# Graph block on one core: bringing the weighted sums back by a scaled reflection on VectorE instead of a transpose and a product on TensorE

## The chip, the core and the metric

The kernel runs on one core of a Trainium2 chip. The metric is the device time of one execution in microseconds. The times given are medians of several runs.

## The reference

64 independent graphs (`B` = 64) of 128 nodes with 128 features each go through two layers. Cut to what matters:

```python
# layer 0, for every pair (i, j) of nodes
h = relu(hi[:, :, None, :] + hj[:, None, :, :] + b1)      # hi = x W1[:H], hj = x W1[H:]
y = einsum('bijk,kl->bijl', h, W2) + b2
y = layernorm(y) * gamma + beta
out0 = einsum('bij,bijh->bih', adj, y)
x1 = layernorm(x + out0)
# layer 1: attention
Wh = x1 @ Ww.T + Wb
s = (Wh @ aw[:C])[:, :, None] + (Wh @ aw[C:])[:, None, :] + ab
e = exp(s) * adj;  alpha = e / sum(e)
x2 = layernorm(x1 + alpha @ x1)
```

Most of the work is the product of 128 x 128 pairs with `W2` for each graph.

## The kernel before

**Slots.** The kernel is a software pipeline of 66 slots. Slot t does three things at once: the pairs of graph t (`pairs`), the weighted sums of graph t-1 (`gather`) and the tail of graph t-2 (`tail`: residual, first layer norm, attention, second layer norm, store); it also prepares graph t+1 (`prep`). The first 12 slots are written out, then a loop of five turns has a body of 10 slots, and the last 4 are written out again (`run_slots`, lines 152 to 161). Each engine runs the same slots in an order written out by hand; semaphores join them. No planner is involved. SyncE's queue issues the loads and stores (lines 181 to 197).

**Units and quarts.** A slot has 16 units, and a unit has two quarts (k = 0 to 31 in a slot), each of four of the 128 rows i. For a unit GpSimd adds the two hidden halves to `h` (line 260), ScalarE applies the relu in place (line 289), two units ahead of the copies, TensorE multiplies each row by `w_pair` into a bank of `y_ps` (lines 606 to 615, a helper `mm` at line 531 issues one product over four column groups, 8 matmul records each), ScalarE copies the quart to `y` (line 371), and VectorE multiplies bank and copy and accumulates the sum of squares in `q` (line 521). `y_ps` has `YRING` = 5 banks, so TensorE begins quart k only when `q_done` tells that quart k-5 is through (line 612).

**The basis.** `w_pair` maps to a basis (a reflection) in which the mean over features falls away: 127 columns carry the centred vector, and the last is the product with the centred second bias. In `y` the last column holds a constant 2, so the squares in line 521 give the variance with the bias in it, and the last column of the weighted sums is twice the sum of the weights, by which the bias comes back. The sums are therefore also in that basis: 32 products of 512 columns, in 8 chunks issued behind the units named in `SUM_AT` (4, 6, 7, 9, 10, 12, 13, 15), land in `agg_ps`.

**The tail before.** VectorE combines the four parts of `agg_ps` to `o_sb` in four steps (lines 450 and 454, unit 0). TensorE transposes it at unit 3 (line 591), ScalarE copies the transpose to `oT_sb` at unit 3 (line 335), and TensorE multiplies by `w_back` at unit 5 (line 594), which brings it back to 128 features with gamma applied. VectorE adds `x_beta` (line 461, unit 5) to get `x1p`, then takes statistics. The rest follows at units 7 (normalise and the two scores), 9 (exponential, scaled copy), 11 (attention product and its use), 12 and 14 (second layer norm). Preparation of the next graph has transposes at unit 7, copies at unit 9, and products and `project` at unit 11.

In the VectorE loop a unit has four places e = 0 to 3, and after each place follow two squares: places 0 and 1 belong to the unit's first quart, 2 and 3 to its second. So place (1, 3) is ahead of the last two squares of quart 3. The steps that the prediction names by a pair (unit, place) are in the function that starts at line 428.

Of the kernel before, what the change touches and what calls it, by code (L numbers as in the profile page):

```python
# [33 lines left out]
def gnn_pair_kernel(nc, x, adj, W1, b1, W2, b2, gamma, beta, Ww, Wb, aw, ab, out):  # L34
# [22 lines left out]
    CHUNK = 4  # L57
# [5 lines left out]
    with ctx:  # L63
# [18 lines left out]
        basis, basis_half = sb("basis", [K, K]), sb("basis_half", [K, K])  # L82
        b2c, b2c_rep = sb("b2c", [K, 1]), sb("b2c_rep", [K, S])
        gdiag = sb("gdiag", [K, K])
        a1rep, a2rep, wbrep, a12 = sb("a1rep", [K, S]), sb("a2rep", [K, S]), sb("wbrep", [K, S]), sb("a12", [K, 1])
        w_pair = sb("w_pair", [K, K])
        w_back = sb("w_back", [K, K])
# [24 lines left out]
        o_sb, oT_sb = sb("o_sb", [S, K]), sb("oT_sb", [K, S])  # L112
# [14 lines left out]
        x2p = att_ps[:, 3 * K:4 * K]  # L127

# [13 lines left out]
        agg_done, o_part, o_stored, oT_ps_s, oT_sb_s, f_ps_s = sem("agg_done"), sem("o_part"), sem("o_stored"), sem("oT_in_psum"), sem("oT_in_sbuf"), sem("f_in_psum")  # L142
# [126 lines left out]
        def _(act):  # L269
# [37 lines left out]
            def slot(t, half, p, pairs, prep, gather, tail, early, first_bank):  # L307
                for u in range(UNITS):
# [69 lines left out]
        def _(dve):  # L378
# [28 lines left out]
            nc.vector.tensor_copy(basis_half[:, 0:LAST], basis[:, 0:LAST]).then_inc(s_setup_dve, 1)  # L407
            nc.vector.tensor_scalar(basis_half[:, LAST:S], basis[:, LAST:S], 0.5, None, ALU.mult).then_inc(s_setup_dve, 1)
# [12 lines left out]
            dve.wait_ge(s_setup_pe, 8)  # L421
            nc.vector.tensor_copy(bnorm[:], att_ps[:, 1:2]).then_inc(s_ready, 1)
            nc.vector.tensor_copy(w_pair[:], agg_ps[:, 0:K]).then_inc(s_ready, 1)
            nc.vector.tensor_copy(w_back[:], agg_ps[:, K:2 * K]).then_inc(s_ready, 1)
            dve.wait_ge(s_ready, 6)
            dve.wait_ge(s_part, 1)

            def slot(t, half, p, pairs, prep, gather, tail, early, first_bank):

                for u, e in ((u, e) for u in range(UNITS) for e in range(2 * QPU)):  # L430
# [13 lines left out]
                    if tail and (u, e) == (0, 0):  # L444

                        dve.wait_ge(agg_done, (t - 1) * CHUNKS)
                        if early >= 3:

                            dve.wait_ge(oT_ps_s, t - 2)
# [12 lines left out]
                    if tail and (u, e) == (5, 1):  # L462
                        dve.wait_ge(x1p_ready, t - 1)
                        nc.vector.bn_stats(st1[:], x1p).then_inc(st1_ready, 1)
                    if tail and (u, e) == (5, 2):
# [4 lines left out]
                    if tail and (u, e) == (7, 0):  # L470
# [3 lines left out]
                    if tail and (u, e) == (7, 1):  # L474
                        nc.vector.tensor_tensor_reduce(out=s_terms[:, 1, :], in0=x1p, in1=v1row[:], scale=rs1[:, 0:1], scalar=0.0,
                                                       op0=ALU.mult, op1=ALU.add, accum_out=s_ij[:, 0:1]).then_inc(si_ready, 1)
                    if tail and (u, e) == (7, 2):
                        nc.vector.tensor_tensor_reduce(out=s_terms[:, 0, :], in0=x1p, in1=v2row[:], scale=rs1[:, 0:1], scalar=score_c[:, 0:1],
                                                       op0=ALU.mult, op1=ALU.add, accum_out=s_ij[:, 1:2]).then_inc(sj_ready, 1)
                    if prep and (u, e) == (11, 0):  # L480
# [4 lines left out]
                    if tail and (u, e) == (11, 0):  # L485
# [3 lines left out]
                    if tail and (u, e) == (11, 1):  # L489
                        dve.wait_ge(z_e_ready, t - 1)  # L490
                        nc.vector.reciprocal(z_r, z_e).then_inc(z_r_ready, 1)
                    if tail and (u, e) == (11, 2):
                        dve.wait_ge(z_r_ready, t - 1)
                        nc.vector.tensor_scalar(rz[:], z_r, e_ij[:, 0:1], None, ALU.mult).then_inc(rz_ready, 1)
                    if tail and (u, e) == (11, 3):
# [4 lines left out]
                    if tail and (u, e) == (12, 0):  # L500
                        dve.wait_ge(x2p_ready, t - 1)
                        nc.vector.bn_stats(st2[:], x2p).then_inc(st2_ready, 1)
                    if tail and (u, e) == (12, 1):
# [4 lines left out]
                    if tail and (u, e) == (14, 0):  # L508
# [22 lines left out]
        def _(pe):  # L531
# [38 lines left out]
            mm(agg_ps[:, K:2 * K], basis_half[:], gdiag[:]).then_inc(s_setup_pe, 1)  # L570


            pe.wait_ge(s_ready, 6)
# [76 lines left out]
```

## Time and profile before

| | |
|---|---|
| median of 3 runs | 2393.05 us (2391.15 to 2393.16) |
| profiled execution | 2389.61 us |
| its span, first to last instruction | 2387.6 us |
| mean granted clock of TensorE | 0.996 |
| TensorE busy | 2349.4 us (98%), 73280 matmul records |
| VectorE busy | 2108.2 us (88%) |
| ScalarE busy | 2200.3 us (92%) |
| GpSimd busy | 2015.2 us (84%) |
| DMA engines, mean share | below 10% in every slice |

The profile is of one execution. Busy time is the union of an engine's instructions; instructions of one engine can overlap, so the distance from one start to the next can be smaller than a duration. A wait is idle time of an engine together with what ended it; "issue" means that the profile shows nothing that it waited for. Timelines give start, duration, engine, line and operation, with neighbours of one kind merged into one row.

### The profile page before, as it was taken

How to read it: one execution, taken by the hardware profiler on the slowest of the kernel's cores; microseconds unless marked ns; L12 is line 12 of the kernel's file. 1: busy time of each engine (PE TensorE's matmuls, PEld its weight loads, DVE VectorE, ACT ScalarE, POOL GpSimd, SP SyncE). 2: the span in 40 equal slices, each digit the busy share in tenths (PEclk: the TensorE clock that was granted, in tenths of full speed). 3: DMA queues.
4: the chain of work that ended last, by engine and by line, in shares of the span. 5: the costliest groups of instructions: out<-in, count | busy, mean ns of one | idle time of the engine just before them, and what ended most of it. 6: DMA issues, size and time to landing. Idle time of an engine off the chain costs nothing.

```text
span 2387.6 us, 179792 instructions
## 1 busy us (share of the span) xinstructions
PE 2349.4 (98%) x73280; PEld 2118.9 (89%) x73280; DVE 2108.2 (88%) x17881; ACT 2200.3 (92%) x3841; POOL 2015.2 (84%) x1227
## 2 busy tenths in 40 slices
PE   8999999999999999999999999999999999999997
PEld 7888888899898899889889889989999889999996
DVE  7898998888898888888889899888898888888897
ACT  7999999999999899999899999989999989999996
POOL 8888888888888888888788888888888878888884
PEclk9999999999999999999999999999999999999999
DMA  0000000000000000000000000000000000000000
GB/s 20 10 15 16 10 16 16 11 16 16 11 16 10 17 16 10 16 12 15 17 11 16 14 12 16 11 17 16 11 16 12 15 17 10 16 16 10 16 9 11
DMA packets 48651, 33.06 MB, mean 14 GB/s; under 512 B 6208, under 2 KB 47808, under 8 KB 47808
## 3 DMA queue, kind: packets, MB, share of 16 engines
q1 hardware_dynamic: 46512, 21.12, 3.2%
q8 instruction: 590, 9.67, 1.7%
q14 instruction: 253, 2.07, 0.3%
q10 hardware_dynamic: 1296, 0.20, 0.0%
HBM read 17.11 MB, written 4.19 MB: 9 GB/s over the span
## 4 chain that ended last, share of the span: by engine, by line
PE 96%; ACT 2%; DVE 1%; issue 1%; POOL 0%; ACTq 0%; DMA 0%; DVEq 0%
PE y_ps L535 74%; PE agg_ps L580 18%; PE prep_ps L535 4%; ACT y L271 1%; ACT h L289 1%; PE att_ps L535 1%; DVE squares L521 0%; POOL h L260 0%; DMA beta_rows<-in_L_gnn_beta_dram 0%; DVE o_sb L454 0%; DVE q L521 0%; POOL wz L251 0%; ACT x1s L354 0%; DVE x1e L472 0%; DVE att_ps L498 0%
## 5 line engine op out<-in xcount | busy, mean ns | idle before, releaser
L260 POOL TENSOR_TENSOR h<-bT,aT 128x1024 f32<-128x1024 f32 x1024 | 1942.4, 1916 | 319.2 <-PE y_ps L535 303.6
L521 DVE CUSTOM_DVE_ANT_0 squares<-y_ps,y 128x128 bf16<-128x128 f32 x8192 | 1848.8, 285 | 219.9 <-ACT y L271 199.2
L535 PEld LDWEIGHTS y_ps<-w_pair,h 128*32 128x32 f32 x65536 | 1894.0, 110 | 160.3 <-issue 108.0
L535 PE MATMUL y_ps<-w_pair,h 128*32 128x128 f32 x65536 | 1961.6, 273 | 17.1 <-issue 11.5
L271 ACT ACTIVATE y<-y_ps 128x508 f32<-128x508 f32 x2048 | 1142.8, 598 | 138.0 <-PE y_ps L535 130.6
L289 ACT ACTIVATE h<-h 128x1024 f32<-128x1024 f32 x1024 | 1092.0, 1066 | 18.3 <-POOL h L260 15.9
L521 DVE DVE_READ_ACCUMULATOR2_ANT q<- 128x1 f32 x8192 | 678.6, 83 | 0.0
L580 PE MATMUL agg_ps<-y,wz 128*32 128x512 f32 x4096 | 583.8, 592 | 0.0
L580 PEld LDWEIGHTS agg_ps<-y,wz 128*32 128x32 f32 x4096 | 173.6, 110 | 3.4 <-issue 3.0
L454 DVE SCALAR_TENSOR_TENSOR o_sb<-agg_ps,part,o_sb 128x128 f32<-128x128 f32 x192 | 66.5, 347 | 0.2
L234 POOL TENSOR_TENSOR wz<-adjT,rstd 128x128 f32<-128x128 f32 x64 | 34.4, 538 | 33.4 <-ACT rstd L323 33.4
L535 PEld LDWEIGHTS prep_ps<-ident,x_in 128*32 128x32 f32 x512 | 26.4, 110 | 29.1 <-issue 23.3
L513 DVE TENSOR_SCALAR x_out<-att_ps,mv,rs 128x128 f32<-128x128 f32 x64 | 26.2, 410 | 28.1 <-ACT rs L360 28.1
L535 PEld LDWEIGHTS prep_ps<-w_back,oT_sb 128*32 128x32 f32 x512 | 26.1, 110 | 27.4 <-issue 20.2
L535 PEld LDWEIGHTS prep_ps<-xT,w1a 128*32 128x32 f32 x512 | 26.4, 111 | 26.1 <-issue 20.3
L246 POOL TENSOR_TENSOR x_beta<-beta_part,x_res 128x128 f32<-128x128 f32 x64 | 29.4, 460 | 9.8 <-ACT beta_part L329 9.8
L535 PE MATMUL att_ps<-x1s,adjS 128*32 128x129 f32 x512 | 32.4, 276 | 3.6 <-ACT x1s L354 3.5
L535 PE MATMUL prep_ps<-ident,o_sb 128*32 128x128 f32 x512 | 31.4, 273 | 4.3 <-DVE o_sb L454 4.3
L535 PE MATMUL prep_ps<-ident,x_in 128*32 128x128 f32 x512 | 32.2, 275 | 3.1 <-DMA x_in<-in_x_dram 3.1
L535 PE MATMUL prep_ps<-w_back,oT_sb 128*32 128x128 f32 x512 | 32.0, 273 | 0.4 <-ACT oT_sb L271 0.4
L535 PE MATMUL prep_ps<-ident,adj_in 128*32 128x128 f32 x512 | 32.2, 275 | 0.0
L535 PE MATMUL prep_ps<-xT,w1b 128*32 128x128 f32 x512 | 32.2, 275 | 0.0
(89 smaller groups left out, 709.9 us busy)
## 6 DMA issues: line engine op xcount, KB each, us to landing
x_in<-in_x_dram SPq DMA_DIRECT2D x64, 64.0 KB, 2.6
adj_in<-in_adj_dram SPq DMA_DIRECT2D x64, 64.0 KB, 2.6
x_res<-in_x_dram SPq DMA_DIRECT2D x64, 64.0 KB, 2.1
adj_res<-in_adj_dram SPq DMA_DIRECT2D x64, 64.0 KB, 2.0
out_dram<-x_out SPq DMA_DIRECT2D x64, 64.0 KB, 1.8
w<-in_L_gnn_W_dram ACTq DMA_DIRECT2D x1, 64.0 KB, 2.4
w1a<-in_L_gnn_W_dram SPq DMA_DIRECT2D x1, 64.0 KB, 2.2
w1b<-in_L_gnn_W_dram SPq DMA_DIRECT2D x1, 64.0 KB, 2.3
```

What stands on the lines that cost most here:

```text
L234: nc.gpsimd.tensor_tensor(columns, adjT[:, 1 - p, :].rearrange("j (g c s) -> j g c s", g=GROUPS, s=CHUNK), rstd[:].rearrange("j (c s g) -> ...
L246: nc.gpsimd.tensor_tensor(x_beta[:], beta_part[:], x_res[:, p, :], ALU.add).then_inc(x_beta_ready, 1)
L260: nc.gpsimd.tensor_tensor(h[:, u % HRING].rearrange("k (r g) s -> k r g s", g=GROUPS), bT[:, p, :].unsqueeze(1).unsqueeze(1).broadcast_to( ...
L271: return nc.scalar.activation(dst, src, ACT.Copy)
L289: nc.scalar.activation(h[:, u % HRING], h[:, u % HRING], ACT.Relu).then_inc(h_ready, 1)
L454: nc.vector.scalar_tensor_tensor(out=o_sb[:], in0=agg_ps[:, e * K:(e + 1) * K], scalar=part[:, e:e + 1], in1=o_sb[:], op0=ALU.mult, op1=AL ...
L513: nc.vector.tensor_scalar(x_out[:], x2p, mv2[:, 0:1], rs2[:, 0:1], ALU.subtract, ALU.mult).then_inc(out_ready, 1)
L521: last = nc.vector.tensor_tensor_reduce(out=squares[:, (first_bank + k) % YRING, n, :], in0=y_ps[(first_bank + k) % YRING][:, n, :], in1=y ...
L535: last = nc.tensor.matmul(dst[cols], lhsT[:, cols], rhs, start=True, stop=True, tile_position=(0, g * GROUP))
L580: last = nc.tensor.matmul(agg_ps[g * GROUP:(g + 1) * GROUP, :], wz[:, g, chunk, :], y_chunk[:, :, g, :], start=(chunk == 0), stop=(chunk = ...
```

## The change

The sums are brought back on VectorE. The basis is a reflection, so going back is the vector itself, plus multiples of two fixed row vectors: the product with gamma (`gamma_rows`, whose last column is zero), `mean_rows` times the sum of the row (`o_sum`), and `bias_rows` times the last column. The fourth combining step writes to PSUM (`o_all`, the place of `x2p`) and also accumulates `o_sum`. Three steps follow at (1, 1), (1, 2) and (1, 3), each waiting for the one before. The transpose, the copy `oT_sb`, the product by `w_back` and their semaphores go. The tail after that stands one unit earlier, preparation two units earlier (transposes at 5, copies at 7, products at 9), and setup builds the three row tiles instead of `w_back`.

```diff
@@ VectorE, setup @@
-            nc.vector.tensor_copy(basis_half[:, 0:LAST], basis[:, 0:LAST]).then_inc(s_setup_dve, 1)
-            nc.vector.tensor_scalar(basis_half[:, LAST:S], basis[:, LAST:S], 0.5, None, ALU.mult).then_inc(s_setup_dve, 1)
+            nc.vector.memset(gamma_rows[:, LAST:S], 0.0).then_inc(s_setup_dve, 1)
+            nc.vector.memset(o_sum[:], 0.0).then_inc(s_setup_dve, 1)
...
-            nc.vector.tensor_copy(w_back[:], agg_ps[:, K:2 * K]).then_inc(s_ready, 1)
-            dve.wait_ge(s_ready, 6)
+            nc.vector.tensor_copy(gamma_rows[:, 0:LAST], agg_ps[:, 2 * K:3 * K - 1]).then_inc(s_ready, 1)
+            nc.vector.tensor_scalar(mean_rows[:, 0:LAST], agg_ps[:, 2 * K:3 * K - 1], -1.0 / (K - sqrt(K)), None, ALU.mult).then_inc(s_ready, 1)
+            nc.vector.tensor_scalar(mean_rows[:, LAST:S], agg_ps[:, 3 * K - 1:3 * K], 1.0 / sqrt(K), None, ALU.mult).then_inc(s_ready, 1)
+            dve.wait_ge(s_ready, 8)
+            nc.vector.scalar_tensor_tensor(out=bias_rows[:], in0=agg_ps[:, K:2 * K], scalar=0.5, in1=mean_rows[:],
+                                           op0=ALU.mult, op1=ALU.subtract).then_inc(s_ready, 1)
+            dve.wait_ge(s_ready, 9)
@@ VectorE, slot @@
-                        nc.vector.scalar_tensor_tensor(out=o_sb[:], in0=agg_ps[:, e * K:(e + 1) * K], scalar=part[:, e:e + 1],
-                                                       in1=o_sb[:], op0=ALU.mult, op1=ALU.add).then_inc(
-                                                           o_stored if e == CHUNK - 1 else o_part, 1)
-
-                    if tail and (u, e) == (5, 0):
+                        if e < CHUNK - 1:
+                            nc.vector.scalar_tensor_tensor(out=o_sb[:], in0=agg_ps[:, e * K:(e + 1) * K], scalar=part[:, e:e + 1],
+                                                           in1=o_sb[:], op0=ALU.mult, op1=ALU.add).then_inc(o_part, 1)
+                        else:
+                            nc.vector.scalar_tensor_tensor(out=o_all, in0=agg_ps[:, e * K:(e + 1) * K], scalar=part[:, e:e + 1],
+                                                           in1=o_sb[:], op0=ALU.mult, op1=ALU.add,
+                                                           accum_out=o_sum[:, 0:1]).then_inc(o_stored, 1)
+                    if tail and (u, e) == (1, 1):
+                        dve.wait_ge(o_stored, t - 1)
+                        nc.vector.tensor_tensor(x1p, o_all, gamma_rows[:], ALU.mult).then_inc(scaled_ready, 1)
+                    if tail and (u, e) == (1, 2):
+                        dve.wait_ge(scaled_ready, t - 1)
+                        nc.vector.scalar_tensor_tensor(out=x1p, in0=mean_rows[:], scalar=o_sum[:, 0:1], in1=x1p,
+                                                       op0=ALU.mult, op1=ALU.add).then_inc(mean_added, 1)
+                    if tail and (u, e) == (1, 3):
+                        dve.wait_ge(mean_added, t - 1)
+                        nc.vector.scalar_tensor_tensor(out=x1p, in0=bias_rows[:], scalar=o_all[:, LAST:S], in1=x1p,
+                                                       op0=ALU.mult, op1=ALU.add).then_inc(bias_added, 1)
+
+                    if tail and (u, e) == (4, 0):
                         dve.wait_ge(x_beta_ready, t - 1)
-                        dve.wait_ge(f_ps_s, t - 1)
-                        nc.vector.tensor_tensor(x1p, tail_ps[:, 1, :], x_beta[:], ALU.add).then_inc(x1p_ready, 1)
+                        dve.wait_ge(bias_added, t - 1)
+                        nc.vector.tensor_tensor(x1p, x1p, x_beta[:], ALU.add).then_inc(x1p_ready, 1)
@@ ScalarE, slot @@
-                    if tail and u == 3:
-                        act.wait_ge(oT_ps_s, t - 1)
-                        if early >= 3:
-
-                            act.wait_ge(f_ps_s, t - 2)
-                        copy(oT_sb[:], tail_ps[:, 0, :]).then_inc(oT_sb_s, 1)
-                    if tail and u == 7:
+                    if tail and u == 6:
...
-                    if prep and u == 9:
+                    if prep and u == 7:
...
-                    if tail and u == 9:
+                    if tail and u == 8:
...
-                    if tail and u == 14:
+                    if tail and u == 13:
@@ TensorE, slot @@
-                    if tail and u == 3:
-                        pe.wait_ge(o_stored, t - 1)
+                    if prep and u == 5:
                         if gather:
 
                             pe.wait_ge(ln_v_ready, t)
-                        mm(tail_ps[:, 0, :], o_sb[:], ident[:]).then_inc(oT_ps_s, 1)
-                    if tail and u == 5:
-                        pe.wait_ge(oT_sb_s, t - 1)
-                        mm(tail_ps[:, 1, :], oT_sb[:], w_back[:]).then_inc(f_ps_s, 1)
-                    if prep and u == 7:
-                        if tail:
-
-                            pe.wait_ge(x1p_ready, t - 1)
                         prep_transposes(t + 1, 1 - p, nth16(half, p, 1), True)
-                    if prep and u == 11:
+                    if prep and u == 9:
                         prep_products(t + 1)
-                    if tail and u == 11:
+                    if tail and u == 10:
```

The other VectorE places move with them: statistics from unit 5 to 4, normalisation and scores from 7 to 6, `project` from 11 to 9, the use of the attention product from 11 to 10, the second statistics from 12 to 11, the output from 14 to 13.

## Rows read from the trace of the kernel before

**Rows 1.** The page: busy time by engine; shares of the chain of waits.
```profile
PE 2349.4 (98%) x73280; PEld 2118.9 (89%) x73280; DVE 2108.2 (88%) x17881; ACT 2200.3 (92%) x3841; POOL 2015.2 (84%) x1227
...
PE 96%; ACT 2%; DVE 1%; issue 1%; POOL 0%; ACTq 0%; DMA 0%; DVEq 0%
```

**Rows 2.** Waits, whole run: total us, times, longest us.
```profile
DVE squares L521 <- ACT y L271: 199.2, 467, 4.3
...
PEld y_ps L535 <- DVE q L521: 15.1, 47, 3.1
```

**Rows 3.** Timeline of TensorE's matmuls in one slot: start us, us, then the instruction.
```profile
1002.68 5.43 PE L535 MATMUL y_ps<-w_pair,h 128*32 128x128 f32 x192
1007.92 0.41 PE L535 MATMUL prep_ps<-ident,o_sb 128*32 128x128 f32 x8
1008.13 3.68 PE L535 MATMUL y_ps<-w_pair,h 128*32 128x128 f32 x128
...
1012.49 0.41 PE L535 MATMUL prep_ps<-w_back,oT_sb 128*32 128x128 f32 x8
1012.71 3.68 PE L535 MATMUL y_ps<-w_pair,h 128*32 128x128 f32 x128
...
1039.02 3.25 PE L535 MATMUL y_ps<-w_pair,h 128*32 128x128 f32 x112
```

**Rows 4.** Timeline of VectorE in the same slot, quarts 1 to 4.
```profile
1006.49 0.34 DVE L454 SCALAR_TENSOR_TENSOR o_sb<-agg_ps,part,o_sb 128x128 f32<-128x128 f32 x1
1006.75 0.28 DVE L521 CUSTOM_DVE_ANT_0 squares<-y_ps,y 128x128 bf16<-128x128 f32 x1
...
1008.85 0.28 DVE L521 CUSTOM_DVE_ANT_0 squares<-y_ps,y 128x128 bf16<-128x128 f32 x1
1009.05 0.08 DVE L521 DVE_READ_ACCUMULATOR2_ANT q<- 128x1 f32 x1
1009.53 0.29 DVE L521 CUSTOM_DVE_ANT_0 squares<-y_ps,y 128x128 bf16<-128x128 f32 x1 [0.39 <-ACT y L271]
```

**Rows 5.** VectorE, same slot: steps like the new ones; then a group.
```profile
1015.28 0.29 DVE L461 TENSOR_TENSOR att_ps<-prep_ps,x_beta 128x128 f32<-128x128 f32 x1
1015.50 0.29 DVE L521 CUSTOM_DVE_ANT_0 squares<-y_ps,y 128x128 bf16<-128x128 f32 x1
...
1020.86 0.41 DVE L478 CUSTOM_DVE_ANT_0 s_terms<-att_ps,v2row,score_c 128x128 f32<-128x128 f32 x1
1021.19 0.08 DVE L478 DVE_READ_ACCUMULATOR2_ANT s_ij<- 128x1 f32 x1
...
L498 DVE SCALAR_TENSOR_TENSOR att_ps<-att_ps,rz,x1e 128x128 f32<-128x128 f32 x64 | 22.7, 354 | 0.1
```

**Rows 6.** Timeline: a read that releases TensorE in slot 0; later, a weight load.
```profile
26.90 0.08 DVE L521 DVE_READ_ACCUMULATOR2_ANT q<- 128x1 f32 x1
27.03 1.75 PEld L535 LDWEIGHTS y_ps<-w_pair,h 128*32 128x32 f32 x64 [0.16 <-DVE q L521]
...
1007.81 0.24 PEld L535 LDWEIGHTS prep_ps<-ident,o_sb 128*32 128x32 f32 x8
```

**Rows 7.** Timeline of TensorE and VectorE in a slot near 898 us.
```profile
897.52 2.89 PE L535 MATMUL y_ps<-w_pair,h 128*32 128x128 f32 x96
...
898.49 0.08 DVE L521 DVE_READ_ACCUMULATOR2_ANT q<- 128x1 f32 x1
```

**Rows 8.** Timeline of TensorE and VectorE in the slot after a loop turn.
```profile
1195.02 3.68 PE L535 MATMUL y_ps<-w_pair,h 128*32 128x128 f32 x128
...
1194.78 0.08 DVE L521 DVE_READ_ACCUMULATOR2_ANT q<- 128x1 f32 x1
```

**Rows 9.** Timeline of VectorE: the last read of quart 8.
```profile
1014.44 0.08 DVE L521 DVE_READ_ACCUMULATOR2_ANT q<- 128x1 f32 x1
```

**Rows 10.** Timeline of VectorE in the first of the two last tails.
```profile
2367.44 0.27 DVE L442 TENSOR_REDUCE adj_sum<-adj_res 128x1 f32<-128x128 f32 x1
2369.22 0.30 DVE L461 TENSOR_TENSOR att_ps<-prep_ps,x_beta 128x128 f32<-128x128 f32 x1 [1.50 <-PE prep_ps L535]
```

More of the change, by code:

```diff
@@ L81, in gnn_pair_kernel @@
         house, centre = sb("house", [K, K]), sb("centre", [K, K])
-        basis, basis_half = sb("basis", [K, K]), sb("basis_half", [K, K])
+        basis = sb("basis", [K, K])
         b2c, b2c_rep = sb("b2c", [K, 1]), sb("b2c_rep", [K, S])
         gdiag = sb("gdiag", [K, K])
+        gamma_rows, mean_rows, bias_rows = sb("gamma_rows", [S, K]), sb("mean_rows", [S, K]), sb("bias_rows", [S, K])
         a1rep, a2rep, wbrep, a12 = sb("a1rep", [K, S]), sb("a2rep", [K, S]), sb("wbrep", [K, S]), sb("a12", [K, 1])
         w_pair = sb("w_pair", [K, K])
-        w_back = sb("w_back", [K, K])
         v1row, v2row = sb("v1row", [S, K]), sb("v2row", [S, K])
@@ L111, in gnn_pair_kernel @@
         part = sb("part", [S, CHUNK])
-        o_sb, oT_sb = sb("o_sb", [S, K]), sb("oT_sb", [K, S])
+        o_sb, o_sum = sb("o_sb", [S, K]), sb("o_sum", [S, 1])
         x1e = sb("x1e", [S, K + 1])
@@ L127, in gnn_pair_kernel @@
         x2p = att_ps[:, 3 * K:4 * K]
+        o_all = x2p
         s_w, s_w1 = sem("weights_loaded"), sem("first_layer_weights_loaded")
@@ L141, in gnn_pair_kernel @@
         v_ready, ln_v_ready, rstd_ready, w_ready, adjS_ready = sem("v_ready"), sem("ln_v_ready"), sem("rstd_ready"), sem("w_ready"), sem("adjS_ready")
-        agg_done, o_part, o_stored, oT_ps_s, oT_sb_s, f_ps_s = sem("agg_done"), sem("o_part"), sem("o_stored"), sem("oT_in_psum"), sem("oT_in_sbuf"), sem("f_in_psum")
+        agg_done, o_part, o_stored = sem("agg_done"), sem("o_part"), sem("o_stored")
+        scaled_ready, mean_added, bias_added = sem("scaled_by_gamma"), sem("mean_part_added"), sem("bias_part_added")
         x1p_ready, st1_ready, mv1_ready, ln1_ready, rs1_ready = sem("x1p_ready"), sem("st1_ready"), sem("mv1_ready"), sem("ln1_ready"), sem("rs1_ready")
@@ L419, in _ @@
             nc.vector.tensor_tensor(score_c[:], setup_ps[:, 3, 0:1], abc[:], ALU.add).then_inc(s_ready, 1)
-            dve.wait_ge(s_setup_pe, 8)
+            dve.wait_ge(s_setup_pe, 9)
             nc.vector.tensor_copy(bnorm[:], att_ps[:, 1:2]).then_inc(s_ready, 1)
             nc.vector.tensor_copy(w_pair[:], agg_ps[:, 0:K]).then_inc(s_ready, 1)
-            nc.vector.tensor_copy(w_back[:], agg_ps[:, K:2 * K]).then_inc(s_ready, 1)
-            dve.wait_ge(s_ready, 6)
+            nc.vector.tensor_copy(gamma_rows[:, 0:LAST], agg_ps[:, 2 * K:3 * K - 1]).then_inc(s_ready, 1)
[5 more added lines that the diff above has]
+            dve.wait_ge(s_ready, 9)
             dve.wait_ge(s_part, 1)
@@ L446, in slot @@
                         dve.wait_ge(agg_done, (t - 1) * CHUNKS)
-                        if early >= 3:
-                            dve.wait_ge(oT_ps_s, t - 2)
                         nc.vector.tensor_scalar(o_sb[:], agg_ps[:, 0:K], part[:, 0:1], None, ALU.mult).then_inc(o_part, 1)
@@ L462, in slot @@
-                    if tail and (u, e) == (5, 1):
+                        dve.wait_ge(bias_added, t - 1)
+                        nc.vector.tensor_tensor(x1p, x1p, x_beta[:], ALU.add).then_inc(x1p_ready, 1)
+                    if tail and (u, e) == (4, 1):
                         dve.wait_ge(x1p_ready, t - 1)
                         nc.vector.bn_stats(st1[:], x1p).then_inc(st1_ready, 1)
-                    if tail and (u, e) == (5, 2):
+                    if tail and (u, e) == (4, 2):
                         dve.wait_ge(st1_ready, t - 1)
@@ L469, in slot @@
                         nc.vector.bn_aggr(mv1[:], st1[:]).then_inc(mv1_ready, 1)
-                    if tail and (u, e) == (7, 0):
+                    if tail and (u, e) == (6, 0):
                         dve.wait_ge(rs1_ready, t - 1)
                         nc.vector.tensor_scalar(x1e[:, 0:K], x1p, mv1[:, 0:1], rs1[:, 0:1], ALU.subtract, ALU.mult).then_inc(x1_ready, 1)
-                    if tail and (u, e) == (7, 1):
+                    if tail and (u, e) == (6, 1):
                         nc.vector.tensor_tensor_reduce(out=s_terms[:, 1, :], in0=x1p, in1=v1row[:], scale=rs1[:, 0:1], scalar=0.0,
                                                        op0=ALU.mult, op1=ALU.add, accum_out=s_ij[:, 0:1]).then_inc(si_ready, 1)
-                    if tail and (u, e) == (7, 2):
+                    if tail and (u, e) == (6, 2):
                         nc.vector.tensor_tensor_reduce(out=s_terms[:, 0, :], in0=x1p, in1=v2row[:], scale=rs1[:, 0:1], scalar=score_c[:, 0:1],
                                                        op0=ALU.mult, op1=ALU.add, accum_out=s_ij[:, 1:2]).then_inc(sj_ready, 1)
-                    if prep and (u, e) == (11, 0):
+                    if prep and (u, e) == (9, 0):
                         if early >= 1:
@@ L484, in slot @@
                         project(t + 1, 1 - p)
-                    if tail and (u, e) == (11, 0):
+                    if tail and (u, e) == (10, 0):
                         dve.wait_ge(att_done, t - 1)
@@ L488, in slot @@
                         nc.vector.tensor_scalar(z_e, att_ps[:, K:K + 1], e_ij[:, 0:1], None, ALU.mult).then_inc(z_e_ready, 1)
-                    if tail and (u, e) == (11, 1):
+                    if tail and (u, e) == (10, 1):
                         dve.wait_ge(z_e_ready, t - 1)
                         nc.vector.reciprocal(z_r, z_e).then_inc(z_r_ready, 1)
-                    if tail and (u, e) == (11, 2):
+                    if tail and (u, e) == (10, 2):
                         dve.wait_ge(z_r_ready, t - 1)
                         nc.vector.tensor_scalar(rz[:], z_r, e_ij[:, 0:1], None, ALU.mult).then_inc(rz_ready, 1)
-                    if tail and (u, e) == (11, 3):
+                    if tail and (u, e) == (10, 3):
                         dve.wait_ge(rz_ready, t - 1)
@@ L499, in slot @@
                                                        op0=ALU.mult, op1=ALU.add).then_inc(x2p_ready, 1)
-                    if tail and (u, e) == (12, 0):
+                    if tail and (u, e) == (11, 0):
                         dve.wait_ge(x2p_ready, t - 1)
                         nc.vector.bn_stats(st2[:], x2p).then_inc(st2_ready, 1)
-                    if tail and (u, e) == (12, 1):
+                    if tail and (u, e) == (11, 1):
                         dve.wait_ge(st2_ready, t - 1)
@@ L507, in slot @@
                         nc.vector.bn_aggr(mv2[:], st2[:]).then_inc(mv2_ready, 1)
-                    if tail and (u, e) == (14, 0):
+                    if tail and (u, e) == (13, 0):
                         dve.wait_ge(rs2_ready, t - 1)
@@ L569, in _ @@
             mm(agg_ps[:, 0:K], w2T[:], basis[:]).then_inc(s_setup_pe, 1)
-            mm(agg_ps[:, K:2 * K], basis_half[:], gdiag[:]).then_inc(s_setup_pe, 1)
-            pe.wait_ge(s_ready, 6)
+            mm(agg_ps[:, K:2 * K], b2c_rep[:], gdiag[:]).then_inc(s_setup_pe, 1)
+            mm(agg_ps[:, 2 * K:3 * K], ones[:], gdiag[:]).then_inc(s_setup_pe, 1)
+            pe.wait_ge(s_ready, 9)
             def weighted_sums(b_parity, chunk):
```

## The prediction

> **What bounds the kernel now.** I read the busy shares and the chain of waits first [rows 1], then the table of who waited for whom [rows 2], then one steady slot as a timeline, TensorE first [rows 3], then VectorE [rows 4].
>
> TensorE is busy for 98% of the span and makes 96% of the chain [rows 1]. Its own waits for VectorE are small: 15.1 us of weight loads held by `q` [rows 2]. The slot of 1002.68 to 1039.02 takes 36.34 us [rows 3]. In it 24 block products of `y_ps` run from 1002.68 to 1007.92, so one block product (8 matmul records) costs 5.24 / 24 = 0.218 us, and a quart of four costs 0.873 us. The two products that the change removes stand in that slot at 1007.92 (0.21 us to the next) and 1012.49 (0.22 us) [rows 3]. So the slot is filled by TensorE, and work taken out of it is worth its full time, as long as nothing else is late.
>
> The reader has to see what could be late. The ring has 5 banks: quart k may start only when VectorE has finished the squares of quart k-5 (`q_done`, line 612). VectorE needs four squares at 0.21 us, 0.84 us a quart, against 0.873 us on TensorE. In units 0 to 3 there are no weighted sums on TensorE (`SUM_AT` begins at 4), so VectorE cannot catch up there, and just there it has the extra steps at the slot's start. From 1006.49 to 1009.05 it starts one instruction after the other with no idle time, and only before 1009.53 does it wait, 0.39 us, for ScalarE's copy of `y` [rows 4].
>
> Quart 3's last accumulator read is at 1009.05 and lasts 0.08, ends 1009.13 [rows 4]. Quart 8, which waits for it, starts at 1008.13 + 2 x 0.873 = 1009.88 [rows 3]. The slack is 0.75 us. Quart 9 starts at 1010.75, and quart 4, from 1009.53, ends 0.84 + 0.08 later, at 1010.46: slack 0.29 us.
>
> **What is removed.** Per tail two block products, 0.218 + 0.218 = 0.437 us of TensorE: the first stood before quart 6, the second before quart 10. Over the 62 slots that have both a tail and pairs (2 to 63) this is 27 us, if nothing takes their place. ScalarE's copy to `oT_sb` goes too; I cost it at nothing, because quart 8 waits for VectorE work that has no ScalarE wait in front of it.
>
> **What is added.** Three VectorE steps at (1,1), (1,2), (1,3), all ahead of the end of quart 3's squares. What counts is the distance from one start to the next. The product with `gamma_rows`: line 461 has the same kinds of operands, and the squares follow it 0.22 us later (1015.28 to 1015.50) [rows 5]. The two scalar_tensor_tensor: the one at 1006.49 is followed 0.26 us later (1006.75) [rows 4]. Sum 0.22 + 0.26 + 0.26 = 0.74 us. Two things have no row. The fourth weighted-sum step now also accumulates `o_sum`; squares accumulate at 0.21 us, so nearly nothing is expected, and the ends are 0 and the read's 0.08. The last step takes its scalar from PSUM; a second pointer made line 478 0.33 (1020.86 to 1021.19), 0.07 over 0.26 [rows 5], so its ends are 0 and 0.07. I take 0.77, with ends 0.63 (three at the 0.21 of a square) and 0.94 (0.77 plus both, rounded).
>
> The Trainium skill, "VectorE: DVE Perf Modes", section "The DRAIN you can't avoid", speaks against the change: it says that the next operation does not start until the pipe is empty. By that rule each step would cost its whole duration; the rival below prices it. The rows disagree so far: 0.35 long, the next start 0.26 later.
>
> **The new wait.** Quart 3's squares end 0.77 later, and quart 8 is ready 0.218 earlier. A stalled quart also needs time to begin: after the read of 26.90 ended at 26.98 the weight load started at 27.03, 0.05 later, and a matmul follows its load by 0.11 (load at 1007.81 [rows 6], matmul at 1007.92 [rows 3]); 0.16 together. Stall before quart 8: 0.77 + 0.218 + 0.16 - 0.75 = 0.40 us. Quart 9 adds nothing: quart 4's squares can start at 1009.05 + 0.77 = 1009.82 rather than 1009.53, end 0.29 later at 1010.75, and quart 9 in its new place, 1009.88 - 0.218 + 0.40 + 0.873 = 1010.93, is later than that by 0.18. Queued behind the stalled quart on TensorE is everything else of the slot, so the stall counts in full.
>
> The slot then changes by -0.437 + 0.40 = -0.04 us. In other slots the slack is smaller: in the one around 898 us, 60 of the 64 records of quarts 6 and 7 are left at 897.52, so quart 8 starts at 897.52 + 60 x 0.0273 = 899.16, and the read ends at 898.57 (0.0273 is 0.218 / 8) [rows 7]: slack 0.59, stall 0.56, the slot 0.12 us longer. Some slots have TensorE late on its own queue, which the new stall partly swallows. I take the 57 ordinary slots (62 less the five after a loop turn) at zero.
>
> The first slot after each of the five loop turns is different: quart 8 starts at 1195.02 + 1.746 = 1196.77 and the read ends at 1194.86 [rows 8], slack 1.9 us. No stall; these give the whole 0.437: 2.2 us.
>
> **What is moved.** Statistics, scores, preparation and attention go one or two units earlier on all engines together, and the transposes now stand before quart 10, giving 0.437 us there that they take back at 14. The first step that they could hurt is quart 13: it starts at 1012.71 + 2.62 = 1015.33 and needs the read of 1014.44, ended 1014.52 [rows 9], slack 0.8. TensorE is there 0.40 us later than before (the removed 0.437 returned by the transposes, plus the stall) and two of the moved steps add some 0.4 us before that read, of which VectorE's wait hides a part. So it stays at 0.8. From there on a weighted sum stands between most quarts, and the slack grows. I cost the moves at nothing; if that cover went, they would cost the 0.4 us. No DMA is issued differently, but the loads of `x_in` and `adj_in` on SyncE's queue start earlier, since they wait for the transposes; their data is needed a slot later.
>
> Setup: one more product and about 0.7 us more of VectorE before TensorE's first quart. The first squares wait for ScalarE and GpSimd anyway; nothing. The last two tails: `x1p` came at 2369.22, 1.78 us after the reduction began at 2367.44 [rows 10]. Now it follows that reduction by three dependent steps of some 0.4 us: 0.3 us less at best.
>
> **Sum.** 0 + 2.2 + 0.3 = 2.5 us less. The profiled execution took 2389.61, a span of 2387.6 and 2.0 around it; the median of the runs is 2393.05, 0.14% above, and I take the difference over unchanged: 2390.5 us.
>
> **The rivals.**
> A, the whole 27 us arrives: it needs VectorE's delay to disappear before quart 3 ends. 62 x 0.437 = 27, so 2366. For it: TensorE is 98% busy. Against it: VectorE's unbroken row of starts [rows 4]. Chance 0.07.
> B, the steps are cheap, near 0.63 us: stall 0.26, 0.18 x 57 = 10 and 2.5, so 2380.5. Chance of a gain over 4.8 us this way 0.15.
> C, slower: the steps hold VectorE for as long as their bars are. One of line 498 lasts 0.354 [rows 5], line 461's 0.29: 0.29 + 0.35 + 0.35 = 1.0 us, stall 0.63, the slot 0.19 us longer, 57 x 0.19 = 11 less the 2.5: 2401.5. It decides for slower by 0.2% once the three cost more than 0.90 us. With the dear ends only (0.94) it gives 0.13 x 57 - 2.5 = 5, 2398. It is what the rule of the Trainium skill on the drain ("VectorE: DVE Perf Modes", "The DRAIN you can't avoid") would do here. Chance 0.20.
> D, the change does not do what it says, since the new place of `x1s` or of the moved copies on ScalarE makes TensorE wait later in the slot: 0.2 us a slot would be 11 us, 2402. Nothing in units 8 to 15 is that close. Chance 0.02.
>
> **How the numbers follow.** A measurement of this kernel tells about 0.2%, 4.8 us, from no change. The forecast, within that of the old time, has 0.56, A and B 0.22, C and D 0.22. The range takes in the ends of the step costs, B and C: 2380 to 2402. It leaves out A.
>
> **What would show it.** After the change: the two products gone and the quarts still at 0.873 us; the three steps 0.22 and 0.26 apart from what follows; a new wait of TensorE for `q` before quart 8, some 0.3 to 0.5 us, in most slots; slots of about 36.3 us, those after a turn 0.4 us shorter. If the wait is absent and slots are 35.9, A is right. If the steps' spacing is 0.3 to 0.35, C. The prediction is wrong in its working if slots are shorter or longer by a wait in another place.

## The result, and the profile after

The changed kernel takes 2374.19 us (2370.8 to 2379.49, 5 runs); the kernel before 2391.15 us (2386.97 to 2393.16, 5 runs). The ratio is 0.9935, interval 0.9916 to 0.9953: faster by 0.65%, about 15 us. The prediction of 2390.5 us, range 2380 to 2402, was wrong, and the time lies below its range. The profiled execution of the changed kernel took 2375.56 us, span 2373.6, clock 0.995; before 2389.61 and 2387.6. The spans differ by 14.0 us. The five executions of the changed kernel lie up to 8.7 us apart, so what follows from one profiled execution of each kernel holds to a few us in all; only the floors defined below repeat to 0.01 us.

The page, as in [rows 1]:

```profile
PE 2328.1 (98%) x72264; PEld 2008.4 (85%) x72264; DVE 2147.3 (90%) x18140; ACT 2191.7 (92%) x3777; POOL 2017.4 (85%) x1227
...
PE 76%; DVE 16%; issue 5%; ACT 3%; ACTq 0%; DMA 0%; DVEq 0%
```

VectorE has moved into the chain, from 1% to 16%. The table of waits alone does not show the new wait: weight loads held by `q` went from 15.1 us, 47 times [rows 2], to 43.9 us, 140 times, but the kernel without the three steps, tried below, has 50.4 us, 170 times, and no wait before quart 8. The timeline shows it.

One steady slot of the changed kernel on TensorE (timeline: start us, us, instruction), to set beside [rows 3]:

```profile
997.68 9.20 PE L548 MATMUL y_ps<-w_pair,h 128*32 128x128 f32 x320
1006.69 1.04 PE L594 MATMUL agg_ps<-y,wz 128*32 128x512 f32 x8
...
1033.87 2.37 PE L548 MATMUL y_ps<-w_pair,h 128*32 128x128 f32 x80
```

The slot takes 1033.87 - 997.68 = 36.19 us. Its first 320 records, ten quarts, take 9.01 us until the weighted sum; at 0.873 us a quart they would take 8.73. So 0.28 us of waiting lie in there, 0.26 before quart 8 and 0.02 behind it. VectorE in the same slot, to set beside [rows 4]:

```profile
1001.49 0.35 DVE L456 SCALAR_TENSOR_TENSOR att_ps<-agg_ps,part,o_sb 128x128 f32<-128x128 f32 x1
1001.76 0.14 DVE L456 DVE_READ_ACCUMULATOR att_ps<-agg_ps,part,o_sb 128x1 f32 x1
1001.76 0.28 DVE L534 CUSTOM_DVE_ANT_0 squares<-y_ps,y 128x128 bf16<-128x128 f32 x1
...
1002.80 0.29 DVE L461 TENSOR_TENSOR att_ps<-att_ps,gamma_rows 128x128 f32<-128x128 f32 x1
1003.00 0.28 DVE L534 CUSTOM_DVE_ANT_0 squares<-y_ps,y 128x128 bf16<-128x128 f32 x1
...
1003.42 0.35 DVE L464 SCALAR_TENSOR_TENSOR att_ps<-mean_rows,o_sum,att_ps 128x128 f32<-128x128 f32 x1
1003.68 0.28 DVE L534 CUSTOM_DVE_ANT_0 squares<-y_ps,y 128x128 bf16<-128x128 f32 x1
...
1004.10 0.35 DVE L468 SCALAR_TENSOR_TENSOR att_ps<-bias_rows,att_ps 128x128 f32<-128x128 f32 x1
1004.36 0.28 DVE L534 CUSTOM_DVE_ANT_0 squares<-y_ps,y 128x128 bf16<-128x128 f32 x1
...
1004.78 0.08 DVE L534 DVE_READ_ACCUMULATOR2_ANT q<- 128x1 f32 x1
```

And TensorE just behind that read, its matmuls in one view and its weight loads in another:

```profile
1004.92 1.30 PE L548 MATMUL y_ps<-w_pair,h 128*32 128x128 f32 x40
...
1004.92 1.14 PEld L548 LDWEIGHTS y_ps<-w_pair,h 128*32 128x32 f32 x44 [0.34 <-DVE q L534]
```

The read ends at 1004.86, and quart 8 begins 0.06 us later. The wait is where the prediction put it.

**Where the 14.0 us went.** I measured every slot as the distance between the first matmuls of quart 0 in successive slots, and call the shortest slot of a kernel its floor. The loop has five turns, so it jumps back four times; each jump lengthens the slot that it ends and the one behind it, eight slots in all. The other 42 slots of the loop are ordinary, and what they have over the floor in all is called their gaps.

| us | before | after | difference |
|---|---|---|---|
| start, slots 0 and 1 | 84.5 | 84.7 | +0.2 |
| slots 2 to 11, written out | 363.4 | 363.1 | -0.4 |
| 42 ordinary slots of the loop | 1536.8 | 1520.9 | -15.9 |
| of these the floor, 42 x 36.343 and 42 x 36.185 | 1526.4 | 1519.8 | -6.6 |
| of these gaps | 10.4 | 1.1 | -9.3 |
| 8 slots at the jumps | 308.1 | 310.2 | +2.1 |
| end | 94.8 | 94.7 | -0.1 |

Two things stand out: the floor fell by 0.158 us instead of the 0.04 forecast for the steady slot, and the gaps are gone. In the kernel before, a gap looks like this on TensorE, here in three slots that are ten apart:

```profile
530.53 0.96 PE L535 MATMUL y_ps<-w_pair,h 128*32 128x128 f32 x27 [0.45 <-issue]
...
900.87 0.96 PE L535 MATMUL y_ps<-w_pair,h 128*32 128x128 f32 x27 [0.46 <-issue]
...
1271.09 0.96 PE L535 MATMUL y_ps<-w_pair,h 128*32 128x128 f32 x27 [0.17 <-issue]
```

All three stand behind the fourth of the 32 records of quart 9, at the same instruction of the loop body in three turns. Inside a quart the kernel has no wait, and the profile names none.

### The profile page after: what moved, and what is told of

The parts are those of the page before. It is cut to its first block, busy times and chain, and to the rows that moved or that the text cites. A ratio compares the mean times of both kernels' runs of the same rounds, so it can differ in the third digit from the quotient of the medians.

```text
span 2373.6 us, 177761 instructions
## 1 busy us (share of the span) xinstructions
PE 2328.1 (98%) x72264; PEld 2008.4 (85%) x72264; DVE 2147.3 (90%) x18140; ACT 2191.7 (92%) x3777; POOL 2017.4 (85%) x1227
## 4 chain that ended last, share of the span: by engine, by line
PE 76%; DVE 16%; issue 5%; ACT 3%; ACTq 0%; DMA 0%; DVEq 0%
PE y_ps L548 56%; PE agg_ps L594 16%; DVE squares L534 9%; PE prep_ps L548 2%; DVE q L534 2%; ACT y L273 2%; ACT h L291 1%; DVE att_ps L456 1%; DVE o_sb L453 1%; DVE att_ps L468 1%; DVE att_ps L464 1%; PE att_ps L548 1%; DVE o_sb L448 1%; DVE att_ps L461 0%; DVE adj_sum L443 0%
## 5 line engine op out<-in xcount | busy, mean ns | idle before, releaser
L548 PEld LDWEIGHTS y_ps<-w_pair,h 128*32 128x32 f32 x65536 | 1821.7, 110 | 263.0 <-issue 208.1
L548 PE MATMUL y_ps<-w_pair,h 128*32 128x128 f32 x65536 | 1922.5, 273 | 22.8 <-issue 13.9
L594 PE MATMUL agg_ps<-y,wz 128*32 128x512 f32 x4096 | 537.3, 592 | 2.8 <-DVE att_ps L456 2.8
L594 PEld LDWEIGHTS agg_ps<-y,wz 128*32 128x32 f32 x4096 | 127.9, 110 | 7.1 <-POOL wz L236 3.6
L548 PEld LDWEIGHTS att_ps<-x1s,adjS 128*32 128x32 f32 x512 | 17.8, 110 | 44.6 <-issue 35.5
L453 DVE SCALAR_TENSOR_TENSOR o_sb<-agg_ps,part,o_sb 128x128 f32<-128x128 f32 x128 | 44.3, 346 | 0.1
L437 DVE TENSOR_SCALAR prep_ps<-q,bnorm 128x128 f32<-128x128 f32 x64 | 22.6, 354 | 10.4 <-issue 8.2
L485 DVE TENSOR_SCALAR x1e<-att_ps,mv,rs 128x128 f32<-128x128 f32 x64 | 26.2, 410 | 3.9 <-ACT rs L337 1.9
L331 ACT ACTIVATE beta_part<-beta_rows,adj_sum 128x128 f32<-128x128 f32 x64 | 25.5, 398 | 3.8 <-DVE adj_sum L443 3.8
L350 ACT ACTIVATE x1s<-x1e,e_ij 128x129 f32<-128x129 f32 x64 | 25.9, 405 | 2.1
```

Source lines behind the costliest of these rows:

```text
L485: nc.vector.tensor_scalar(x1e[:, 0:K], x1p, mv1[:, 0:1], rs1[:, 0:1], ALU.subtract, ALU.mult).then_inc(x1_ready, 1)
L548: last = nc.tensor.matmul(dst[cols], lhsT[:, cols], rhs, start=True, stop=True, tile_position=(0, g * GROUP))
L594: last = nc.tensor.matmul(agg_ps[g * GROUP:(g + 1) * GROUP, :], wz[:, g, chunk, :], y_chunk[:, :, g, :], start=(chunk == 0), stop=(chunk = ...
```

## The experiments

Theories on the floor: the ring before quart 8 (the three steps delay quart 3's squares), against something else in the slot. Theories on the gaps: A, the new wait swallows them; B, they depend on TensorE's instructions, by their count, their place in the slot or their address; C, chance. Where only one execution is given, its sum of gaps is uncertain by 2 us or so (10.4 and 12.1 us in two executions of the kernel before).

### The kernel before once more

> The kernel before, looked at once more. In its first profile the 56 ordinary slots sum to 2051.8 us with a median slot of 36.34, so 16.5 us lie over the median, most of it gaps of TensorE that the profile puts to issue. Theory own queue (gaps belong to this program): about 10 to 17 us over the median again, most gaps before quarts 6 to 10. Rival chance (gaps differ from execution to execution): anything from 0 to 17, in other slots.

Span 2390.1 us. Gaps 12.1 us, jumps 307.3. The gaps belong to the program, and so do their places. To see where they fall I compared every ordinary slot with a usual one, matmul record by matmul record. In the first execution 21 stalls are longer than 0.15 us, 8.4 of the 10.4 us. They stand at nine places of the loop body, and eight of these show again in the second execution, as the one shown above does:

```profile
902.38 0.96 PE L535 MATMUL y_ps<-w_pair,h 128*32 128x128 f32 x27 [0.17 <-issue]
```

All 21 stand within 5 records of a regular grid, one place every 125 matmul records, counted from the start of the loop body; most places of the grid show none. Which turn has a stall, and how long it is, differs. Chance (C) falls.

### The change without its three steps

```diff
-                    if tail and (u, e) == (1, 1):
...
-                    if tail and (u, e) == (1, 3):
...
-                        dve.wait_ge(bias_added, t - 1)
-                        nc.vector.tensor_tensor(x1p, x1p, x_beta[:], ALU.add).then_inc(x1p_ready, 1)
+                        dve.wait_ge(o_stored, t - 1)
+                        nc.vector.tensor_tensor(x1p, o_all, x_beta[:], ALU.add).then_inc(x1p_ready, 1)
```

> The changed kernel without the three VectorE steps; leaves out bringing the sums back. Ring theory: the wait before quart 8 goes and the median slot is 35.90 (36.34 less 0.437). If another step of the slot held the changed kernel, the slot stays at 36.2. On the gaps of TensorE's own queue: theory A, the wait before quart 8 swallows them: they come back here, some 10 us over the median, span about 2361. Theory B, they went with the fewer TensorE instructions or with their place in memory: they stay away, span about 2351.

2359.28 us, ratio 0.9853 (0.9834 to 0.9871), span 2356.0. Floor 35.91: the three steps are the whole of what holds the changed kernel above the full removal, and the ring theory stands. The span lies midway between the two forecasts, 2361 and 2351; the gaps decide. They are 1.1 us, with no wait before quart 8. So no wait swallowed them, and A falls.

### The kernel before with three steps

```diff
...
+                    if tail and (u, e) == (1, 1):
+                        nc.vector.tensor_tensor(x1p, x2p, ones[:], ALU.mult).then_inc(d1_ready, 1)
+                    if tail and (u, e) == (1, 2):
+                        dve.wait_ge(d1_ready, t - 1)
+                        nc.vector.scalar_tensor_tensor(out=x1p, in0=ident[:], scalar=part[:, 0:1], in1=x1p,
+                                                       op0=ALU.mult, op1=ALU.add).then_inc(d2_ready, 1)
+                    if tail and (u, e) == (1, 3):
+                        dve.wait_ge(d2_ready, t - 1)
+                        nc.vector.scalar_tensor_tensor(out=x1p, in0=ident[:], scalar=x2p[:, LAST:S], in1=x1p,
+                                                       op0=ALU.mult, op1=ALU.add).then_inc(d3_ready, 1)
...
```

> The kernel before with three VectorE steps of the same forms put at (1,1), (1,2), (1,3); their result is not used. Both products on TensorE stay. Ring theory: quart 3 ends 0.73 later against a slack of 0.75 to 0.71 and a wake-up of 0.06 to 0.15, so a wait of 0.05 to 0.15 before quart 8 and slots of 36.40 to 36.50, up to 6 us more in all. Theory A (a wait swallows gaps): TensorE now has no slack to lose, gaps before quarts 6 to 8 hurt less, 16.5 over the median becomes 8 or less, span 2381 to 2386. Theory B: the gaps stay, span 2391 to 2395.

2397.32 us, ratio 1.0007 (0.9997 to 1.0018), span 2395.5. The floor is 36.47 in the written-out slots and 36.39 in the loop, as the ring theory gave. Gaps 14.3 us although there is a wait, if a short one: A falls from this side too, and the span is half a microsecond above B's range.

### The steps spread

```diff
-                    if tail and (u, e) == (1, 1):
+                    if tail and (u, e) == (2, 0):
...
-                    if tail and (u, e) == (1, 2):
+                    if tail and (u, e) == (3, 0):
...
-                    if tail and (u, e) == (1, 3):
+                    if tail and (u, e) == (4, 0):
...
-                    if tail and (u, e) == (4, 0):
+                    if tail and (u, e) == (4, 1):
```

(The statistics follow at (4, 2) and (4, 3).)

> The changed kernel with the same three steps at (2,0), (3,0), (4,0), where VectorE waits for ScalarE's copy anyway, and the addition and statistics one place later, (4,1) to (4,3). Ring theory: quart 3 is no longer delayed, quart 4 by nothing (0.22 fits in its 0.47 us of idle time), so the wait before quart 8 goes; quart 9 is left with 0.29 - 0.218 = 0.07 us; median slot 35.90 to 36.00, 11 to 16 us less than the changed kernel in all. If the count of steps and not their place matters, the slot stays at 36.2. With theory A on the gaps the span is about 2361 to 2364, with B 2351 to 2358.

2361.69 us, ratio 0.9856 (0.9838 to 0.9874), span 2360.6, floor 35.91, gaps 4.4. The span is 13.0 us below that of the changed kernel, as the ring theory said, but above B's range of 2351 to 2358; against the kernel without the steps, 3.3 of the 4.6 us more are gaps. The same three steps cost nothing on the floor when VectorE would be idle. TensorE in one slot:

```profile
991.30 8.92 PE L548 MATMUL y_ps<-w_pair,h 128*32 128x128 f32 x320
1000.04 1.04 PE L594 MATMUL agg_ps<-y,wz 128*32 128x512 f32 x8
```

Ten quarts in 8.74 us: no wait is left. VectorE in the same slot shows why:

```profile
997.68 0.30 DVE L461 TENSOR_TENSOR att_ps<-att_ps,gamma_rows 128x128 f32<-128x128 f32 x1
998.15 0.29 DVE L534 CUSTOM_DVE_ANT_0 squares<-y_ps,y 128x128 bf16<-128x128 f32 x1 [0.17 <-ACT y L273]
```

The first step ends inside VectorE's wait for ScalarE's copy, and 0.17 us of it are still over.

### Two products put back into the changed kernel

```diff
+                    if tail and u == 3:
+                        pe.wait_ge(o_stored, t - 1)
+                        if gather:
+                            pe.wait_ge(ln_v_ready, t)
+                        if pairs:
+                            pe.wait_ge(ab_sb_s, t + 1)
+                        mm(prep_ps[:, 0, :], ones[:], ident[:])
+                    if tail and u == 5:
+                        mm(prep_ps[:, 1, :], ones[:], ident[:])
```

> The changed kernel with two products on TensorE put back at units 3 and 5 (on constants, result unused). Ring theory: quart 8 comes 0.218 later against the same VectorE, so the wait of 0.26 shrinks to 0.04 to 0.13; shortest slot 36.38 to 36.47. Gaps in TensorE's own queue (excess of the 42 slots of the loop body that are not at a jump, over the shortest slot: 10.5 and 12.3 in two looks at the kernel before, 1.3 in the changed one): theory count or place of the products says they return, 8 to 14; theory address says they stay near 1 or land anywhere, since the code around is not that of before.

2402.71 us, one run; span 2400.7. Floor 36.41, gaps 11.8 (expected 8 to 14). The products bring the gaps back. The slots written out are at 36.5 and longer, 366.5 us for the ten, and the jumps take 311.9, so this is slower than either kernel.

### Two products at other units

In the kernel with the spread steps:

```diff
+                    if tail and u in (12, 14):
+                        if prep:
+                            pe.wait_ge(ab_sb_s, t + 2)
+                        mm(prep_ps[:, 0, :], ones[:], ident[:])
```

> The kernel with the spread steps, and two products on TensorE put back, but at units 12 and 14. Shortest slot 35.91 + 0.437 = 36.35. Theory count (more instructions in a slot or in the loop body make the gaps): excess 8 to 14 as before. Theory place (the gaps come since products stand in the long run of quarts without weighted sums, units 0 to 4): excess 1 to 5, as without them.

2389.08 us, one run; span 2386.9. Floor 36.35, gaps 8.3, against 4.4 without the products. They come back although the products are far from the long run of quarts. The theory of place in the slot falls, count stays.

### Code shifted

```diff
             prep_transposes(0, 0, 16, False)
+            for _ in range(10):
+                mm(y_ps[0][:, 0, :], ident[:], ident[:])
```

In the kernel before:

> The kernel before with ten products more in TensorE's setup, in an idle time of it, so that all its later code lies 160 records further on. Setup is not longer by more than 0.5 us. Theory address: the excess of the 42 slots changes clearly from 10.5 to 14.2, to below 6 or above 18. Theories count and place: 9 to 15.

2403.28 us, one run; span 2401.2. Gaps 9.3, within what count expects. But the jumps: the eight slots take 321.5 us instead of 308.1. A jump now shows two waits of TensorE, the second and third line, instead of the one of the kernel before, the first line:

```profile
1187.87 7.11 PE L535 MATMUL y_ps<-w_pair,h 128*32 128x128 f32 x192 [2.41 <-issue]
...
1189.53 0.66 PE L535 MATMUL y_ps<-w_pair,h 128*32 128x128 f32 x8 [2.63 <-issue]
1192.56 7.00 PE L535 MATMUL y_ps<-w_pair,h 128*32 128x128 f32 x184 [2.38 <-issue]
```

And in the change without its steps:

> The kernel without the three steps, shifted in the same way; leaves out bringing the sums back. Theory address: its excess of 1.0 us rises, to over 5. Theories count and place: it stays between 0.5 and 5; shortest slot 35.91.

2363.76 us, one run; span 2361.6. Floor 35.91, gaps 2.6, eight slots at jumps 313.5 instead of 308.2. This one shift of the address moves the price of the jumps and not the sum of the gaps. It does move where they fall: in the shifted kernel before, 19 stalls are longer than 0.15 us, none at a place of the kernel before. They stand on the same grid of 125 records, met 80 records earlier in the loop body, and 80 is what the ten products put ahead of it. The few stalls of the shifted kernel without steps stand on such a grid too. So a gap belongs to an address in TensorE's stream of instructions, and not to a step of the algorithm.

### No loop

```diff
-            for t in range(PEEL):
+            for t in range(LOOP_END):
                 slot(t, t // 2, t % 2, True, True, t >= 1, t >= 2, min(t, 4), t * QUARTS % YRING)
-            with engine.Fori(0, (LOOP_END - PEEL) // BODY) as turn:
-                for s in range(PEEL, PEEL + BODY):
-                    slot(turn * BODY + s, turn * (BODY // 2) + s // 2, s % 2, True, True, True, True, 4, s * QUARTS % YRING)
```

In the kernel before:

> The kernel before with all 66 slots written out, no loop. In every look the 10 written-out slots 2 to 11 stood exactly at the floor (363.43 us in the kernel before), and the gaps of TensorE's own queue and the jumps (10.4 and 17.3 us over the floor of 36.34) were in the loop's slots only. Theory loop (gaps belong to code that is run in a loop): all slots at 36.34, span 2387.6 - 27.7 = 2360. Theory stream (gaps come with the time that the code has been running, written out or not): the jumps go, the gaps stay or grow, span 2370 to 2380.

2365.53 us, ratio 0.9898 (0.9880 to 0.9917). The 42 slots have 2.1 us over the floor, and those that had been at jumps 0.2. Of TensorE's waits for nothing that the profile shows (total us, times, longest us) this is left; the loop's kernel before had 11.5 us in 14 waits, the second fence. Most of those are the jumps: the changed kernel, which has hardly a gap, shows 13.9 us in 7.

```profile
PE y_ps L532 <- issue: 0.5, 2, 0.3
```

```profile
PE y_ps L535 <- issue: 11.5, 14, 2.4
```

In the kernel with the spread steps:

> The kernel with the spread steps, all slots written out. Theory loop: all slots at 35.91, so 2360.6 less 4.4 of gaps and 22.1 of jumps, span 2334. Theory stream: 2334 to 2342.

2337.28 us, ratio 0.9779 (0.9761 to 0.9798), span 2335.7, gaps 1.6 and at the former jumps 0.1. This is the fastest version, 2.2% below the kernel before.

### One product and four

The kernel with the spread steps and the code of the two products at other units, with `u == 14` alone, and with u in 11 to 14.

> The kernel with the spread steps and one product put back on TensorE, at unit 14 (on constants, result unused). Floor 35.91 + 0.218 = 36.13. Theory count, graded: excess of the 42 slots about half way, 4 to 8. Theory count with a step (at one product more or less the supply of instructions no longer keeps up): either 1 to 4.5 as with none, or 8 to 14 as with two.

2380.81 us, one run; span 2378.7. Floor 36.13, gaps 4.1, jumps 316.3. Both theories had 4.1 in their ranges, so this decides nothing.

> The same with four products, at units 11 to 14. Floor 35.91 + 0.873 = 36.79. Theory count, graded: excess of the 42 slots over 14, near 18 to 25. With a step: 8 to 14, as with two. If the count has nothing to do with it, below 5.

2427.28 us, one run; span 2425.3. Floor 36.78, gaps 10.6 (a graded count would give 18 to 25), jumps 319.9. Four products make no more gaps than two.

### The loop begun later

`PEEL` 32 instead of 12.

> The kernel before with slots 0 to 31 written out and the loop of ten slots only from 32 on (three turns, two jumps). Theory loop: slots 12 to 31 at the floor of 36.34 within 2 us in all; slots 32 to 61 (less the four at jumps) have gaps at the rate of the first loop, 10.4 / 42 x 26 = 6 us; two jumps 8.7 us instead of four 17.3. Span about 2387.6 - 27.7 + 6 + 9 = 2375. Theory place in the code or time since start: gaps also in 12 to 31.

2377.43 us, one run; span 2375.6 as forecast, but not by the forecast terms. The written-out slots 12 to 31 have 2.0 us over the floor, the loop's ordinary slots 1.4 instead of 6, and the two jumps cost 12.2 instead of 8.7. So the gaps do not come with two products and a loop wherever that loop begins.

### The changed kernel without a loop

> The changed kernel with all slots written out, to compare with the kernel before written out (2365.53 us). Without the loop only the ring's part of the change is left: written-out slots stood at 36.27 against 36.34, so 62 x 0.07 = 4 us less, about 2361. If the gain of 15 us belonged to the change itself and not to the gaps in the loop, 2350.

2359.45 us, ratio 0.9880 (0.9862 to 0.9898), span 2357.5, floor 36.27. Against the kernel before written out (span 2363.8) it is 6.3 us less by the spans; the two ratios, 0.9880 and 0.9898, differ by no more than their intervals, so the runs alone do not tell it clearly from nothing. The slots say more: the floor is 36.27 against 36.34, and 62 x 0.07 = 4.3 us is the ring's part. It is smaller than in the loop because in all but two of the written-out slots quart 8 begins 0.15 us after the read that releases it, and not 0.06: the wait is 0.36 us instead of 0.26.

## Why the prediction was wrong, point by point

- **What bounds the kernel.** Right: TensorE, at a floor of 36.34 us. Without the steps the floor was 35.91, the 0.437 us to the last hundredth (x2).
- **The steps.** Right, and a little dear: 0.20, 0.26 and 0.26 us apart from what follows, 0.01 for the accumulator read, 0.73 in all against the 0.77 taken. The scalar in PSUM costs no more than one in SBUF. Rival C falls: the next start comes 0.26 us after the start of a step that lasts 0.35. (Its 0.90 us as the point of 0.2% slower does not follow from the prediction's own sum, which reaches 4.8 us at 0.94.) The rule of the Trainium skill ("VectorE: DVE Perf Modes", "The DRAIN you can't avoid"), that the next operation waits for the empty pipe, taken alone would have made C right, and these rows do not bear it out. The same section of the Trainium skill adds that a next operation that is not held starts earlier, and with that the rows agree.
- **The new wait.** Right in place, wrong in size: 0.26 us in the loop, not 0.40. The term that was mis-sized is the wake-up, taken at 0.16. I had it from slot 0, which is written out, and in the written-out slots it is right: 0.15, a wait of 0.36 and a floor of 36.27. In the loop's slots it is 0.06. With 0.73 and 0.06 the sum of the prediction gives 0.73 + 0.218 + 0.06 - 0.75 = 0.26. That is also the stall of rival B, which had it from cheaper steps; its size came, its reason did not. With the 0.02 us behind quart 8 the slot is 0.158 us shorter, and over the 42 ordinary slots this gave the 6.6 us of the floor where I had taken zero.
- **"Some slots have TensorE late on its own queue, which the new stall partly swallows. I take the 57 ordinary slots (62 less the five after a loop turn) at zero."** This is the step that failed. The gaps were 10.4 us, I had seen them in the trace and put them on nobody's account, and they went: 9.3 of the 14.0 us. They weren't swallowed by the stall (x2 has no stall and none of them, x3 has one and all). They follow the two products where the loop begins at slot 12: 8.3 to 14.3 us in six such executions with two of them, 1.1 to 4.4 in the four with none, wherever in the slot they stand. So part of what rival A had claimed arrived, by a mechanism that it did not name.
- **The loop turns.** Wrong twice. There are four jumps, not five, and they did not give 2.2 us but took 2.1. VectorE's slack of 1.9 us was that of one slot; in the four it was 1.1 to 1.9, and in the changed kernel quart 8 still waited for VectorE in two of them (it begins 0.05 us after the read in slots 32 and 52). What those slots wait for most is TensorE's own restart: 17.3 us over the floor in the kernel before, 20.7 in the changed one, 30.7 when ten products moved the code of the kernel before. That the address also made the 3.4 us between the first two is likely from the third, not shown.
- **What is moved, and the ends.** Right for the moves: with the steps out or spread no other wait showed in the floor. The ends did not give the 0.3 us: the start took 0.2 us more and the end 0.1 less.
- **The range.** It took in the uncertain costs of the steps, but not the 10 us of gaps and the 17 us of jumps that stood in the trace. Those are the larger numbers.

**Open.** Why two products more in a slot bring the gaps in the loop, why four bring no more than two, and why a loop that begins at slot 32 has few of them, was not settled. One execution each stands behind the single-run numbers. Shown is that the stalls sit at fixed addresses of TensorE's instructions, 125 matmul records apart, that they move with the code and that they all but vanish when the loop is written out. That they are the supply of instructions falling behind at these places is the likely reading, and no run shows the supply itself.

## What to carry to other kernels

Before costing an edit on the bounding engine, subtract: its floor per iteration, times the count, from the span. What is left over (here 10 us of gaps and 17 us at jumps) can move by more than the edit itself, and it belongs in the range. Extra steps on a second engine cost nothing if each is put where that engine waits anyway: the same three steps cost 0.27 us a slot in one place (36.18 against 35.91) and nothing in another. When a gap has no releaser, look whether it comes back at the same instruction in every turn of the loop. A loop of a program that is bound by TensorE should be tried written out.

## What was not expected of the hardware

- The jump of a loop cost 4 to 8 us each, over two slots, of TensorE's time with nothing named as releaser, and ten products added in setup raised it from 4.3 to 7.7 us.
- Written out, the kernel before was 1.0% faster and the one with spread steps 0.8% faster (ratio 0.9779 against 0.9856).
- A stalled quart of TensorE begins 0.06 us after the end of the read that releases it in the loop's slots, no load time added, and 0.15 us after it in written-out slots, with the loop (slots 2 to 11) or without.
- TensorE's unexplained stalls in the loop stood at addresses 125 matmul records apart, and moved by 80 records with 80 records of code put ahead.
- VectorE's step with an accumulator and one with its scalar in PSUM are each followed after 0.26 to 0.27 us, like the plain one.
